# New engine orders, weight set-up moved in the opening, and narrower spare products, in a kernel of four graph layers

## The reference, cut to what matters

```python
# layer 0: scores from two projections, masked softmax, relu
e = leaky_relu((x@W1) @ (x@W2).T, 0.2);  att = softmax(where(adj > 0, e, -big))
G0 = relu(att @ (x@W3))
# layer 1: scores are a sum of a column and a row
h = x@W;  e = leaky_relu((h@a1)[:, None] + (h@a2)[None, :], 0.2)
G1 = elu(softmax(where(adj > 0, e, -big)) @ h)
# layer 2: mlp1 (256 -> 512), attention without mask (fc), elu and residual,
#          mlp2 (512 -> 256), attention with mask (hand), elu and residual, relu
# layer 3: four heads of 64, q, k, v with biases, masked softmax, output projection wo
```

## Time and profile before

| | us |
|---|---|
| Median of three runs | 2616.76 |
| Profiled execution | 2616.98 |
| Its span, first to last instruction | 2615.2 |
| PE (TensorE) busy | 2525.4 (97%) |
| DVE (VectorE) busy | 2251.1 (86%) |
| ACT (ScalarE) busy | 1968.4 (75%) |
| POOL (GpSimd) busy | 1913.2 (73%) |

### The profile page before, as it was taken

The page is one execution under the profiler, slowest core; times in us unless marked ns, Lnnn a source line. Parts: engine busy times, 40 slices in busy tenths (PEclk is TensorE's granted clock), DMA queues, the critical chain, the costliest instruction groups (busy, mean ns, idle before and its releaser), DMA issues. The chain is left out here.

```text
span 2615.2 us, 64667 instructions
## 1 busy us (share of the span) xinstructions
PE 2525.4 (97%) x21399; PEld 2411.0 (92%) x21399; DVE 2251.1 (86%) x6252; ACT 1968.4 (75%) x4737; POOL 1913.2 (73%) x2439
## 2 busy tenths in 40 slices
PE   6899999999999999999999999999999999999886
PEld 5789999999999999999999999999999999999874
DVE  2478999899999998999999999999989999998874
ACT  2468877887887788778778877877887788787652
POOL 2457877877787877778787777878777787877543
PEclk8899999999999999999999999999999999999998
DMA  4214444444444444444444444344444444443333
GB/s 141 67 52 128 129 142 130 126 139 130 136 123 145 127 126 142 129 138 121 145 126 130 139 134 133 124 142 128 131 134 136 132 128 141 128 132 110 105 106 89
DMA packets 317115, 329.67 MB, mean 126 GB/s; under 512 B 35313, under 2 KB 248689, under 8 KB 316785
## 3 DMA queue, kind: packets, MB, share of 16 engines
q1 hardware_dynamic: 316784, 325.54, 41.5%
HBM read 174.41 MB, written 150.99 MB: 124 GB/s over the span
## 5 line engine op out<-in xcount | busy, mean ns | idle before, releaser
L1234 POOL TENSOR_TENSOR p<-p,rd 128x512 f32<-128x512 f32 x256 | 343.1, 1350 | 5.5
L1159 POOL TENSOR_TENSOR proT_lo<-sco,proT_hi 128x512 fp32r<-128x512 f32 x128 | 165.8, 1295 | 159.7 <-ACT proT_hi L560 159.7
L1171 POOL TENSOR_SCALAR xn<-act,nmean,rstd 128x256 f32<-128x256 f32 x384 | 237.1, 627 | 47.7 <-DVE act L1075 35.3
L786 ACT ACTIVATE p<-p,nmx 128x256 f32<-128x256 f32 x512 | 253.0, 496 | 10.9 <-DVE nmx L1109 10.9
L573 ACT ACTIVATE sco<-sco,nmax 128x256 f32<-128x256 f32 x384 | 192.6, 502 | 40.9 <-DVE nmax L872 36.1
L1181 POOL TENSOR_TENSOR act<-act,x 128x512 f32<-128x512 f32 x64 | 82.9, 1295 | 167.8 <-ACT act L623 167.8
L1109 DVE CUSTOM_DVE_ANT_0 p<-ps,mask 128x256 f32<-128x256 f32 x512 | 188.3, 414 | 15.4 <-PE ps L510 14.0
L872 DVE CUSTOM_DVE_ANT_0 sco<-ps,mask 128x256 f32<-128x256 f32 x384 | 144.9, 414 | 53.2 <-ACT ps L563 41.2
L808 DVE TENSOR_TENSOR xnT_lo<-ps,xnT_hi 128x512 fp32r<-128x512 f32 x192 | 129.7, 675 | 61.0 <-ACT xnT_hi L560 61.0
L1166 POOL TENSOR_TENSOR rstd<-vare,mhalf 128x2 f32<-128x2 f32 x256 | 178.1, 696 | 0.0
L1124 DVE STREAM_TRANSPOSE p<-p 128x1024 f32<-128x1024 f32 x128 | 158.6, 1239 | 18.0 <-POOL p L1234 17.7
(11 more groups left out here) (240 smaller groups left out, 12396.6 us busy)
## 6 DMA issues: line engine op xcount, KB each, us to landing
scratch<-p SPq DMA_DIRECT2D x128, 512.0 KB, 3.0
p4T<-scratch SPq DMA_DIRECT2D x512, 128.0 KB, 3.5
scratch_pro<-act SPq DMA_DIRECT2D x192, 256.0 KB, 2.3
sco<-scratch_pro SPq DMA_DIRECT2D x768, 64.0 KB, 1.9
x0Tp<-in_xT SPq DMA_DIRECT2D x64, 256.0 KB, 2.6
x<-in_x SPq DMA_DIRECT2D x64, 256.0 KB, 2.8
scratch_o<-sco SPq DMA_DIRECT2D x64, 256.0 KB, 2.1
o3r<-scratch_o SPq DMA_DIRECT2D x256, 64.0 KB, 2.5
```

The costliest lines, as they stand in the source:

```text
L786: ins = nc.scalar.activation(rows_, rows_, ACT.Exp, scale=-1.0, bias=nmx4[:, h, m:m + 1], accum_out=den4[:, h, m:m + 1])
L1159: return G.tensor_tensor(lo, whole, hi.bitcast(fp32), ALU.subtract)
L1171: ins = G.tensor_scalar(xn[:, m, :], y[:, m, :], nmean[i][:, m:m + 1], rstd[i][:, m:m + 1], ALU.add, ALU.mult)
L1234: G.tensor_tensor(rows_, rows_, rd4[:, h, :].unsqueeze(2).unsqueeze(3).broadcast_to([P, NT, QUADS, CT * QP]), ALU.mult).then_inc(S["p4n"], 1)
```

## The change

Four things are changed together.

1. ORDERS: the cyclic order of every engine is another one. On PE only two pairs of neighbours change places (`w2`/`v2` and `x1`/`f2`). On ACT, DVE, POOL and SP a dozen steps each stand a few places earlier or later, and the point at which a period begins is another one on some.
2. The first load group holds W1 and W2 alone; W3 and the adjacency matrix have their own semaphore (loaded4). The weights of layer 3 are loaded after x of the second graph.
3. Weight preparation moves: PE makes the columns of layer 1, of hand and of mlp2 ahead of `g0` of graph 1, and those of fc ahead of `a0` of graph 0. VectorE splits W_ ahead of `g0` of graph 1, mlp1 ahead of `h0` of graph 1, fc ahead of `x0` of graph 1, mlp2 and hand ahead of `x0` of graph 2. The four weights of layer 3 are copied to their high parts by ScalarE ahead of its first `a0` (`heads_high`), and their low parts are made by GpSimd ahead of its first `a0` and of its third `l0` (`heads_low`). Only the masks stay on VectorE ahead of `h3`.
4. A spare product is now 128 rows by 128 columns, with a tile of ones as both operands, filled by GpSimd at the start. There are 14 ahead of A0, 8 behind it, 77 in the opening, 185 in the filling and 694 in the closing.

```diff
-    "dv": "... r3:6 h0:0 z3:6 st3:6 r2:4 ag3:6 st0:1 ag0:1 e1:2 o3:5 x1:3 f2:4 t1:2 ...",
+    "dv": "... r3:6 h0:0 z3:6 st3:6 ag3:6 r2:4 e1:2 st0:1 o3:5 ag0:1 t1:2 x1:3 f2:4 ...",
...
-SPARE_FILLING = "r2:0:5 s0:4:3 m2:1:2 d2:0:11 m2:2:2 f3:0:29"
-SPARE_CLOSING = "m3:-5:2 ... a3:-1:19 a4:-2:25 s40:-1:1 s42:-1:5 a4:-1:52 y4:-1:5"
+SPARE_LOADING = 14
+SPARE_FILLING = "r2:0:20 s0:4:16 m2:1:11 d2:0:37 m2:2:11 f3:0:90"
+SPARE_CLOSING = "m3:-5:12 ... a3:-1:49 a4:-2:88 s40:-1:11 s42:-1:20 a4:-1:154 y4:-1:20"
...
+            def busy(b, count):
+                for _ in range(count):
+                    nc.tensor.matmul(ps[:, b, 0:P], ones2[:, :], ones2[:, :], start=True, stop=True)
+            pe.wait_ge(S["setup_pool"], 2)
+            busy(4, SPARE_LOADING)
             pe.wait_ge(S["loaded0"], 16 * n_loads[0])
...
-                    nc.tensor.matmul(ps[:, b, 0:N], WP["W3"][0][:, 0, 0:P], WP["W3"][0][:, 1, :], start=True, stop=True)
+                busy(*spare.get((name, t), (0, 0)))
...
-                {"a0": graph_columns, "h1": made(2), "a1": mixed_columns, "m2": made(3), "n2": made(3), "c2": made(4), "m3": made(5), "q4": made(6), "k4": made(6), "v4": made(6)}, keep_busy)
+                {("h0", 0): made(2), ("g0", 1): graph_columns, ("a0", 0): mixed_columns, ("h1", 0): made(3), ("m2", 0): made(4), ("n2", 0): made(4), ("c2", 0): made(5), ("m3", 0): made(6),
+                 ("q4", 0): heads_made, ("k4", 0): heads_made, ("v4", 0): heads_made}, keep_busy)
...
-                {"x0": made_hidden, "h1": made_mlp1, "x1": made_fc, "c2": made_mlp2, "h3": made_heads})
+                {("g0", 1): made_hidden, ("h0", 1): made_mlp1, ("x0", 1): made_fc, ("x0", 2): made_mlp2, ("h3", 0): head_masks})
...
+            def heads_high():
+                ac.wait_ge(S["loaded3"], 16 * n_loads[3])
+                nc.scalar.activation(W["wqT"], W["wqT"], ACT.Copy, scale=QSCALE).then_inc(S["heads_h"], 1)
+                ac.wait_ge(S["heads_h"], 1)
+                for n in HEAD_WEIGHTS:
+                    copy(WP[n][0][:, :, :], W[n]).then_inc(S["heads_h"], 1)
...
+            def heads_low(i):
+                def step():
+                    for k in (i, i + 1):
+                        n = HEAD_WEIGHTS[k]
+                        po.wait_ge(S["heads_h"], k + 2)
+                        low_part(WP[n][1][:, :, :], W[n], WP[n][0][:, :, :]).then_inc(S["heads"], 1)
+                return step
```

More of the change, by code:

```diff
@@ L43, in run @@
                     ahead(name, k - s)
-                if k == s and name in before:
-                    before[name]()
+                if (name, k - s) in before:
+                    before[name, k - s]()
                 steps[name](k - s)
@@ L220, in later_weights @@
             def later_weights():
-                sp.dma_start(adj_sb, adj).then_inc(S["loaded0"], 16)
+                sp.dma_start(W["W3"], weights["W3"]).then_inc(S["loaded4"], 16)
+                sp.dma_start(adj_sb, adj).then_inc(S["loaded4"], 16)
                 sp.dma_start(ident[:, :], ident_d).then_inc(S["loaded1"], 16)
@@ L237, in load_x0T @@
                     later_weights()
+                if t == 1:
+                    load_weights(3)
             def load_x0(t):
@@ L327, in _ @@
             ins.then_inc(S["setup_pe"], 1)
+            busy(4, 8)
             pe.wait_ge(S["made"], 1)
@@ L333, in graph_columns @@
                     for k in range(CT):
[L334 to L337 removed]
+                        nc.tensor.matmul(bank[6][:, m, 0:2], W["W_T"][:, k, m * P:(m + 1) * P], W["a1"][:, k, :], start=(k == 0), stop=(k == CT - 1))
                 pe.wait_ge(S["loaded2"], 16 * n_loads[2])
[L339 removed]
                 for m in range(CT):
@@ L342, in mixed_columns @@
                         nc.tensor.matmul(bank[7][:, m, 0:2], W["hand_T"][:, k, m * P:(m + 1) * P], W["ahand"][:, k, :], start=(k == 0), stop=(k == CT - 1))
-                for m in range(HT):
-                    for k in range(HT):
-                        nc.tensor.matmul(bank[5][:, 0, 2 * m:2 * m + 2], fcT_tiles[k][:, m * P:(m + 1) * P], W["afc"][:, k, :], start=(k == 0), stop=(k == HT - 1))
                 for m in range(CT):
@@ L349, in mixed_columns, with heads_made @@
                 ins.then_inc(S["setup_pe"], 1)
+            def mixed_columns():
+                for m in range(HT):
+                    for k in range(HT):
+                        ins = nc.tensor.matmul(bank[5][:, 0, 2 * m:2 * m + 2], fcT_tiles[k][:, m * P:(m + 1) * P], W["afc"][:, k, :], start=(k == 0), stop=(k == HT - 1))
+                ins.then_inc(S["setup_pe"], 1)
             def made(n):
                 return lambda: pe.wait_ge(S["made"], n)
+            def heads_made():
+                pe.wait_ge(S["heads"], 4)
             tenants = {}
@@ L832, in _ @@
             split([(A0, slice(0, CT), slice(0, C), A0f[:, :, :])]).then_inc(S["made"], 1)
+            dv.wait_ge(S["loaded4"], 32)
+            split([whole_weight("W3")]).then_inc(S["made"], 1)
+            V.tensor_scalar(mask16[:, :, :], adj_sb, 0.0, MASK, ALU.is_le, ALU.mult)
             def made_hidden():
@@ L866, in made_heads @@
                 V.tensor_scalar(some3[:, :], some3[:, :], 0.0, None, ALU.is_equal)
-                split([whole_weight(n) for n in ("wqT", "wkT", "wvT", "woT")]).then_inc(S["made"], 1)
             def masked(i, whole):
@@ L1155, in _ @@
             G.memset(ones[:, :], 1.0).then_inc(S["setup_pool"], 1)
-            po.wait_ge(S["setup_pool"], 1)
+            G.memset(ones2[:, :].bitcast(fp32), 1.0).then_inc(S["setup_pool"], 1)
+            po.wait_ge(S["setup_pool"], 2)
             def low_part(lo, whole, hi):
```

31 lines of the change are left out of this document (10 added, 21 removed), and 10 rows, old and new, of the table ORDERS.

## The result

The changed kernel takes 2628.11 us (median of 6 runs, 2624.76 to 2631.45), the kernel before 2617.24 us (6 runs): ratio 1.0039, 95% interval 1.0027 to 1.0051. It is slower by 11 us, or 0.4%, which is clear of the noise. Forecast were 2615.5 us, range 2599 to 2627; the case that came closest is the second rival, spares dearer than the lead (2627 us, chance 0.13), and not by its own reason. The profiled execution took 2629.25 us with a span of 2627.4. Further down, one execution each of two kernels was slow beyond all others (4118 and 4918 us); the ratios leave these out.

The account below looks back on a forecast made before the run. TensorE alone bounds the middle, so only opening, filling and closing can win. Opening -8.9, filling 0 and closing +7.6 sum to -1.3 on the profiled 2616.98 us; forecast 2615.5 us, range 2599 to 2627.

Parts of the forecast that it names:

- the second rival: Closing and f3: spares at 0.12 us each cost more than the opening's lead wins; +10.5, 2627 us, chance 0.13.
- Start, -3.6: Opening: A0 waits for W1 and W2 alone, so g0 begins at 9.9 us, not 13.48; -3.6 us.
- Clock of h0 and s0, -1.8: Opening, first graph's h0 and s0: less low clock after less idling; bounds 0 and -4.4, taken as -1.8 us.
- Loads of layer 3, +1.5: Opening: eight load issues and their transfer stand ahead of the first pro_out; bounds 0 and +5, taken as +1.5 us.
- Columns, 0, or +2 at a low clock: Opening: moved weight columns lie in waits ahead of second g0 and first a0; 0, +2 if the clock is low.
- From the first a0 to the first a1: Opening: layer 3 work on ACT and POOL 0, bounds ±2; earlier layer 1 mask on DVE -1.0 at first a1.
- First m2: Opening: the wait for the split of fc goes, -3.1 us, and -0.9 for low clock behind it.
- Filling: Filling: 185 spares cost +3.1, a better clock gives -3.1; f3's 90 spares eat its earlier start; together 0.
- The closing, +7.6: Closing: 682 spares at 0.11 us cost +13.9, less 4.0 hidden in both last a4 and 2.3 of clock.
- The -4.0: Closing, both last a4: overfill hides in part because the second half waits for a later transfer; -4.0 us.
- cheap spares: Filling and closing: spares cost 0.06 to 0.08 us each and fit the gaps; about 2599 to 2603 us, chance 0.20.
- The rival with a wait in every period: Middle: m2's 0.9 us slack overrun by 0.2 us in 55 periods; +11, 2626 us, chance 0.08.

Follow-up runs that it names:

- the closing alone: The changed kernel with fewer spare products in the closing only (448 in place of 682 by the study's count), filling as changed: 2621.94 us, ratio 1.0009.
- the run with the columns back: The changed kernel with the 32 fc columns back ahead of the first a1 and their VectorE split back at the first x1: 2629.18 us, ratio 1.0033.
- changed counts in the kernel before: The kernel before with the changed spare counts in filling and closing, as 128-column products of W3: 2627.48 us, ratio 1.0029.
- changed, old orders: The changed kernel with the five cyclic orders of the kernel before: 2625.05 us, ratio 1.0016.
- both (fitted): The changed kernel with fewer spare products in filling and closing, fitted to the gaps of the kernel before: 2609.75 us, ratio 0.9967.
- none at all: The changed kernel without the spare products of filling and closing, one each left: 2610.39 us, ratio 0.9961.

## Why the prediction was wrong

The two sums, -1.3 forecast and +12.2 measured between the profiled executions, are 13.5 us apart. In the forecast's own terms: by 98 us -8.9 was forecast and -3.5 measured (5.4, the stretch from the first `a0` to the first `a1`); the filling, 0, was +1.8; the middle, 0, was +3.0; the closing, +7.6, was +11.0. For the last two the sum had no term for the new orders. The single terms:

**Start, -3.6:** right (9.89 for the 9.9 worked out). **Clock of h0 and s0, -1.8:** right in kind, -2.6 measured.

**Loads of layer 3, +1.5:** too small. The eight issues took 5.2 us (18.25 to 23.46), one of them 1.84, for the 3.4 worked out. 2.3 us behind the issues and 1.3 of transfer were measured; with the columns, which held `a0` as well, they cost 2.8 us of lead. **Columns, 0, or +2 at a low clock:** the clock was low, 6.8 us for the 32; moved by turns, they were shown to bind as much as the transfer does (columns away: no gain; loads away: no gain; both away with the splits: `a0` 4.0 us earlier). At the first `a0` the sum still held: -3.4 for the -3.9 forecast.

**From the first a0 to the first a1** 4.2 us of lead were lost where the forecast had ±2 for the head weights and -1.0 more lead. The rows show two things there: the heads' five ScalarE steps (35.61 to 38.45 us) and two GpSimd steps (to 40.49) ahead of `h0` and `x0`, with idling of 1.76 and 1.80 us for 0.94 and 1.07; and low clock in 42.0 to 52.2 and 55.6 to 65.8 for 6.8 us of it in the kernel before. The clock is the larger part: the trace of "the closing alone", whose code is the same up to here, has the same two waits (1.78 and 2.38 us) and starts `a0` at 32.28 but the first `a1` at 71.27, not 74.43; its low clock is 27.3 of the first 100 us, not 44.4 (34.1 in the kernel before). Moving the splits alone changed no time. So the step that failed is the lead between `a0` and `a1`, put at -1.0 with ±2 for the splits, and nothing in the sum stood for a clock that falls in this stretch; how much of the 4.2 us another execution would show stays open.

**First m2:** the split of fc is off this wait, and 3.1 us of lead came from the first `a1` to it; the run with the columns back shows the wait again (4.41 us). Right.

**The opening's sum** was -8.9; at 250 us it is -1.7. By 98 us it is -3.5. The filling was called "together 0", and by the trace it was +1.8: the six places took 4.2 us more, and the low clock's 7.8 us of busy time were gone, worth 3.9; 1.5 us more were lost, for the most part at two waits of `m2` behind `f3` (0.90 us at 165.59 and 0.95 us at 191.70) that the kernel before does not have. **Filling:** I wrote that f3 could start 5 us earlier and that its spares eat the gain, and so it came; as a forecast that was right, and it was also the costliest part of the change. Cutting them to 14 gave 9.2 us: the largest single cause. That graph 8 then had 8.85 us of lead, nearly the sum's 8.9, is luck: it came by the spares, not by the sum's terms.

**The closing, +7.6, measured +11.0.** The price was right: 0.112 us for the 0.11 taken, and the load does set it. From the start of `g0` of graph 63 to the last matmul, by adding up the traces (us; spares are counted from the first of a group to the next step, without the idling behind them):

| | spares | idle | other matmuls | sum | mean clock |
|---|---|---|---|---|---|
| before | 27.2 | 41.6 | 195.0 | 263.8 | 0.97 |
| changed counts in the kernel before | 77.7 | 5.3 | 187.6 | 270.7 | 1.00 |
| changed, old orders | 77.7 | 4.8 | 187.9 | 270.4 | 1.00 |
| changed | 78.0 | 8.8 | 188.0 | 274.8 | 1.00 |
| closing alone (fitted) | 54.3 | 20.0 | 195.2 | 269.5 | 0.97 |
| both (fitted) | 53.3 | 19.8 | 191.9 | 265.0 | 0.99 |
| none at all | 0.5 | 61.4 | 204.7 | 266.6 | 0.89 |

The counts alone cost 6.9 us for the 7.6 forecast, with terms that were each off. The places with spares took 16.6 us more (77.7 for 61.1), not 13.9: I counted 682 products in 20 places, there are 694 in 21, the added one ahead of `m3` of graph 61, and each took 0.112. The other idling fell by 2.4 (7.7 to 5.3), not by 4.0, and the other matmuls fell by 7.4 at full clock, not by 2.3. The -4.0 had a wrong reason, too. In both last `a4` 4.1 us of overfill do hide, but not behind a later transfer: the second half waited 0.26 us for it, and 0.24 in the `a4` before. The rest is the clock, which stood at 0.50 there in the kernel before, and the 16 products that took 3.96 us take 1.95 in the changed one:

```profile
2598.70:2605.50 6.80, 4.04 (x17) 1.79 (x17) 0.00 (x0) 0.04 (x1) 0.00 (x0) 0.50 0.71 154
```

```profile
2601.20 1.98 PE L536 MATMUL ps<-p4T,v 128*64 128x256 f32 x8 [6.60 <-DMA p4T<-scratch]
2603.44 1.98 PE L536 MATMUL ps<-p4T,v 128*64 128x256 f32 x8 [0.26 <-DMA p4T<-scratch]
```

What made the forecast of the closing fail is the step from 270.7 to 274.8: 3.1 of these 4.1 us are the new orders' four waits, which no spare touches and for which the sum had no term. The rival "dear spares" gave 2627 for a price of 0.12; the price was 0.112, so its time came near for a reason that was not its own. The rival "cheap spares" falls: in fp32r a pair of load and product with 128 columns each came every 0.110 us, not every 0.06 to 0.08. The 81 ns that the prediction quotes from the Trainium skill (TensorE: Matmul & The Clock Gate, Back-to-back issue gap) were not seen here; the measurement decides.

**The middle, 0:** it is +3.0. The rival with a wait in every period described it, at another place (`s40` for `m2`) and at 0.05 us a period for the 0.2 it assumed: 53 waits, 2.9 us. The one long period at graph 60 and two short jumps, 1.9 us together, are evened out by eight jumps of the kernel before worth 1.9. With the old orders the wait is gone. The prediction had looked at one wait only, that of `m2`. That the last thing to end before `s40` is VectorE's addition at L1118 is read from the trace; it was not tried apart.

**What was wrong as a whole:** the price of a spare was disputed at length, and the counts were only compared with the old waits. I did not ask at each place what the changed kernel would still wait for, nor what the new orders make TensorE wait for. At `f3` the change itself removes the wait that its 90 products were to fill.

## What to carry to other kernels

Filler work must fit in the wait as it is after all other edits, not as it was before them. Build the kernel without filler, read its waits, then set the counts; here none at all was as fast as the best fit, and both 0.7 to 0.8% faster than the counts that came with the change. Where two or three causes end a wait within some tenths of a microsecond, moving one shows nothing; move them together before calling one harmless. And a step moved is not time won: with all three moved `a0` started 4.0 us earlier and the kernel was no faster. Where a stage idles and its clock moves, compare medians of many executions, and read one trace for what waits for what, not for a microsecond or two.

## What the runs showed of the hardware

- A pair of load and product in fp32r takes 0.110 to 0.112 us with 128 weight columns for 32, 64 or 128 streamed columns, 0.061 with 64 weight columns and 128 streamed, 0.033 with 32 and 64: narrow the weights, not the stream, to make it cheap.
- TensorE lost its clock while it was busy without a gap: 88 products with 64 streamed columns went from 0.112 to 0.213 us each within the group, 55 with 32 as well, while 88 with 128 columns at the same place kept 1.00 (one execution each). The 32 columns of fc, two streamed columns each, stood at 0.213 too, over 6.8 us of unbroken work.
- The closing without spare products ran at a mean clock of 0.89 and took 266.6 us; with fitted counts it took 265.0 us at 0.99 and 269.5 us at 0.97.
- Executions of one opening differ: with the same code the low clock took 27.3 to 44.4 of the first 100 us, and the first `m2` started between 88.16 and 91.50 us.
